# Second attention layer: q and k rows turned by VectorE and sent through DRAM in place of TensorE transpositions

## The reference, cut to what matters

```python
q = (hidden_states @ Wq + bq).reshape(b, n, H, HD)     # b = 2, n = 512, H = 32, HD = 128
k = (hidden_states @ Wk + bk).reshape(b, n, H, HD)
v = (hidden_states @ Wv + bv).reshape(b, n, H, HD)
q = rmsnorm(q, gq)                                     # over each head's 128 numbers
k = rmsnorm(k, gk)
scores = jnp.einsum('bnhd,bmhd->bhnm', q, k) * scale
attn = jax.nn.softmax(scores, axis=-1)
out = jnp.einsum('bhnm,bmhd->bnhd', attn, v).reshape(b, n, H * HD)
return out @ Wo + bo
```

## Time and profile before

| | us |
|---|---|
| median of the runs | 2196.71 |
| the profiled execution | 2198.5 |
| its span | 2196.7 |
| first attention layer and what follows it, about | 0 to 840 |
| second attention layer, about | 840 to 1950 |
| last feed-forward, about | 1950 to 2197 |

### The profile page before, as it was taken

The page is one execution under the profiler, slowest core; times in us unless marked ns, Lnnn a source line. Parts: engine busy times, 40 slices in busy tenths (PEclk is TensorE's granted clock), DMA queues, the critical chain, the costliest instruction groups (busy, mean ns, idle before and its releaser), DMA issues. The chain is left out here.

```text
span 2196.7 us, 37916 instructions
## 1 busy us (share of the span) xinstructions
PE 2089.8 (95%) x10535; PEld 1757.2 (80%) x10535; DVE 1636.8 (75%) x2972; ACT 1348.5 (61%) x3637; POOL 1222.3 (56%) x985
## 2 busy tenths in 40 slices
PE   6999999999999879999999999999999999868998
PEld 4788888888888657888888888888888888756786
DVE  6778888888788776778777777777777787775422
ACT  5777777777776455656566565666656665544321
POOL 3878778787786554546454554545445463354300
PEclk9999999999999989999999999999999999979999
DMA  2644444434444513555454455444554444643210
GB/s 83 131 105 126 108 110 114 115 104 127 102 119 129 140 55 69 105 122 114 114 108 104 109 119 115 109 99 111 118 115 111 99 111 93 142 95 105 87 53 25
DMA packets 219135, 231.69 MB, mean 105 GB/s; under 512 B 100528, under 2 KB 130384, under 8 KB 218992
## 3 DMA queue, kind: packets, MB, share of 16 engines
q1 hardware_dynamic: 218992, 229.97, 43.7%
HBM read 114.23 MB, written 6.55 MB: 55 GB/s over the span
## 5 line engine op out<-in xcount | busy, mean ns | idle before, releaser
L90 POOL TENSOR_TENSOR l_probsT_lo<-l_moved,l_probsT_hi 128x512 fp32r<-128x512 f32 (+2 forms) x256 | 280.4, 1100 | 296.7 <-ACT l_probsT_hi L947 269.2
L941 ACT ACTIVATE l_probs<-l_score,l_negtop 128x512 f32<-128x512 f32 x256 | 175.8, 687 | 373.2 <-DVE l_negtop L1052 359.9
L90 DVE TENSOR_TENSOR l_probsT_lo<-l_moved,l_probsT_hi 128x512 fp32r<-128x512 f32 (+1 forms) x256 | 292.5, 1143 | 37.4 <-ACT l_probsT_hi L947 37.0
L1052 DVE TENSOR_REDUCE l_negtop<-l_score 128x1 f32<-128x512 f32 x256 | 175.7, 687 | 93.1 <-PE l_score L85 90.6
L1833 ACT ACTIVATE l_probs<-l_score,l_negtop 128x128 f32<-128x128 f32 (+3 forms) x256 | 134.7, 526 | 170.3 <-DVE l_negtop L1946 169.4
L83 PE MATMUL l_out<-l_w_out_lo,l_oT_hi 128*128 128x512 f32 x512 | 209.0, 408 | 6.2 <-DVE l_oT_lo L1078 4.0
L83 PE MATMUL l_score<-l_kT_lo,l_qT_hi 128*128 128x512 f32 (+3 forms) x512 | 191.0, 373 | 22.4 <-POOL l_qT_lo L90 8.9
L1946 DVE CUSTOM_DVE_ANT_0 l_score<-l_score,l_mask 128x128 f32<-128x128 f32 (+3 forms) x256 | 125.9, 492 | 106.9 <-PE l_score L85 105.5
L84 PE MATMUL l_out<-l_w_out_hi,l_oT_lo 128*128 128x512 f32 x512 | 201.7, 394 | 0.0
L85 PE MATMUL l_out<-l_w_out_hi,l_oT_hi 128*128 128x512 f32 x512 | 201.5, 393 | 0.0
L83 PE MATMUL l_general<-l_w_qk_lo,xT_hi 128*128 128x512 f32 x504 | 198.1, 393 | 2.5 <-PEq L1452 2.5
(11 more groups left out here) (249 smaller groups left out, 6235.7 us busy)
## 6 DMA issues: line engine op xcount, KB each, us to landing
l_moved<-l_blocks SPq DMA_DIRECT2D x1024, 64.0 KB
l_moved<-l_blocks SPq DMA_DIRECT2D x512, 80.0 KB
l_inv_all<-inv_rows SPq DMA_DIRECT2D x32, 512.0 KB
l_raw_out<-l_wo SPq DMA_DIRECT2D x64, 256.0 KB, 4.3
l_inv_all<-inv_rows SPq DMA_DIRECT2D x64, 256.0 KB
l_raw_q<-l_wq SPq DMA_DIRECT2D x32, 256.0 KB, 4.0
l_raw_qk<-l_wq SPq DMA_DIRECT2D x64, 128.0 KB, 2.8
l_raw_qk<-l_wk SPq DMA_DIRECT2D x64, 128.0 KB, 2.9
```

What stands on the lines that cost most here:

```text
L90: return engine.tensor_tensor(out, full, hi.bitcast(F32), ALU.subtract)
L941: act.activation(probs[:, n % NPR], score[n % 2][:], ACT.Exp, bias=negtop[:, n:n + 1], accum_out=total[:, n:n + 1]).then_inc(s_exp, 1)
L1052: dve.tensor_reduce(negtop[:, n:n + 1], score[n % 2][:], AXX, ALU.max, negate=True)\
```

## The change

The eight TensorE uses "tq" and "tk" of a turn go. In their place, per unit: VectorE turns the four scaled y tiles in blocks of 32 x 32 into `y_blocks` (`TURNS1`, steps -7 and -6 of the unit, two each, at the end of VectorE's step). SyncE sends them to a DRAM tensor `y_rows` in four transfers of 256 KB (`SENDS1`, step -5), and takes them back per slot in two transfers of 256 KB in turned order (`TAKES1`, step -4 of an even slot, -5 of an odd one), as soon as all four transfers of the send have landed and TensorE has made the last score that reads the buffer. ScalarE makes the high halves out of the landed rows (`HALVES1`, step -2 or -3) and scales k's rows in place, GpSimd subtracts for the low halves, which lie in the place of the landed rows. In a step, sends and takes stand on SyncE between the biases and `move`. The score product reads the keys through `by_tile`, in runs of 32 numbers, since their order is now another. The first unit's two slots are still turned by TensorE, ahead of the loop, into the banks of scores and outputs (`turn_first`, `first_hi`, `first_lo`). The bias buffer has one place instead of two, so its load waits for the last y tile of the turn before and moves to step -17. Smaller edits: semaphores are shared between uses (in the block before and in the last feed-forward, counts adjusted), and the loads of the last stage wait for the turned rows in place of the last transposition's bank.

```diff
-USES1 |= {(kind, s): 4 * s + n for kind, n in (("tq", -4), ("tk", -3), ("pv", PV_AT)) for s in range(SLOTS)}
-USES1 = Plan(USES1, lambda x: ("y", "v", "tq", "tk", "pv").index(x[0]))
+USES1 |= {("pv", s): 4 * s + PV_AT for s in range(SLOTS)}
+USES1 = Plan(USES1, lambda x: ("y", "v", "pv").index(x[0]))
+TURNS1 = Plan({(r, b, t): 16 * r + 8 * b - 7 + t // 2 for r, b in PAIRS for t in range(TB)}, lambda x: x)
+SENDS1 = Plan({(r, b): 16 * r + 8 * b - 5 for r, b in PAIRS})
+TAKES1 = Plan({(s,): 4 * s - (4, 5)[s % 2] for s in range(SLOTS)})
+HALVES1 = Plan({(kind, s): 4 * s - (2, 3)[s % 2] for kind in QK for s in range(SLOTS)})
...
-BIAS1 = Plan({(r,): 16 * r - 22 for r in range(2)})
-
-
-def of_halved(x):
-    return x[0] in ("v", "tq", "tk")
+BIAS1 = Plan({(r,): 16 * r - 17 for r in range(2)})
...
-        qT = split("qT", [P, 2, S])
-        kT = split("kT", [P, 2, S])
+        with ExitStack() as early:
+            turned = p.sb(early, "l1_turned", [P, 2, 2, S])
+        qk_lo = sb("qk_lo", [P, 2, 2, S], F32R)
+        qT, kT = (Split(sb(f"{kind}T_hi", [P, 2, S], F32R), qk_lo[:, k]) for k, kind in enumerate(QK))
...
+        y_blocks = sb("y_blocks", [P, 4, C, P])
...
+        def first_turned(h, kind):
+            return (score, out_bank)[h][kind == "k"]
...
+        def by_hand(m, d, slot):
+
+            return m.first and d == 0 and slot < 2
...
+        def item_of(x):
+            return turned[:, QK.index(x[0]), x[1] % 2]
+
+        def by_tile(rows):
+            return rows.rearrange("p (g t i) -> p t g i", g=TB, t=TB)
...
+            def send_rows(m, unit, d):
+                if not (m.first and m.number(SENDS1, unit, d) <= 3):
+                    sp.wait_ge(s_y_in, y_taken(m, pair_slots(*unit)[1], d, 4))
+                    sp.nop(nofuse=True)
+                if not (m.first and m.number(SENDS1, unit, d) <= 2):
+                    sp.wait_ge(s_y_sent, y_sent(m, unit, d, 1))
+                    sp.nop(nofuse=True)
+                sp.wait_ge(s_y_block, m.done(TURNS1, (*unit, TB - 1), d) - TB)
+                sp.nop(nofuse=True)
+                for g in range(TB):
+                    sp.dma_start(y_rows[unit[1], g].rearrange("n c i x -> i (n c) x"),
+                                 y_blocks[32 * g:32 * g + 32].rearrange("p n c x -> p (n c) x")).then_inc(s_y_sent, 16)
+
+            def take_rows(m, slot, d):
+                r, b, h = pair_of(slot)
+                sp.wait_ge(s_y_sent, y_sent(m, (r, b), d))
+                sp.nop(nofuse=True)
+                if not (m.first and slot == 2):
+                    sp.wait_ge(s_y_in, y_taken(m, slot, d, 1))
+                    sp.nop(nofuse=True)
+                sp.wait_ge(s_score, (m.i + d) * TILES + TB * (slot - 1))
+                sp.nop(nofuse=True)
+                for k in range(2):
+                    sp.dma_start(turned[:, k, h].rearrange("p (g x) -> p g x", g=TB),
+                                 y_rows[b, :, h + 2 * k].rearrange("g c i x -> (c i) g x")).then_inc(s_y_in, 16)
...
+                    for x, d in m.turns(SENDS1, n):
+                        send_rows(m, x, d)
+                    for x, d in m.turns(TAKES1, n):
+                        if not by_hand(m, d, x[0]):
+                            take_rows(m, x[0], d)
...
-                elif kind in ("tq", "tk"):
-                    r, b, h = pair_of(x[1])
-                    if kind == "tq" and h == 0:
-                        pe.wait_ge(s_yn, m.done(USES1, ("y", r, b, TB - 1), d, of_y))
-                    at = (h + 2 * (kind == "tk")) * HD
-                    for t in range(TB):
-                        last = pe.transpose(bank[:, t * P:(t + 1) * P], y[:, b, t, at:at + HD], ident[:])
...
-                            pe.wait_ge(s_free, m.done(USES1, ("tk", slot)))
+                            pe.wait_ge(s_qk_lo, m.done(HALVES1, ("k", slot)))
                         wait_past(pe, s_exp, m, TILES, n - 1)
-                        product(nc, score[n % 2][:], qT[:, slot % 2, t * P:(t + 1) * P], kT[:, slot % 2])\
+                        keys = Split(by_tile(kT.hi[:, slot % 2]), by_tile(kT.lo[:, slot % 2]))
+                        product(nc, tokens(score[n % 2][:]), qT[:, slot % 2, t * P:(t + 1) * P], keys)\
...
+            def rows_hi(x, m, d):
+                kind, s = x
+                act.wait_ge(s_y_in, y_taken(m, s, d))
+                if kind == "q":
+                    last = act.activation(qT.hi[:, s % 2], item_of(x), ACT.Copy)
                 else:
-                    act.activation(kT.hi[:, x[1] % 2], bank[:], ACT.Copy, scale=gains[:, 2:3]).then_inc(s_bank_hi, 1)
+                    act.activation(kT.hi[:, s % 2], item_of(x), ACT.Copy, scale=gains[:, 2:3])
+                    last = act.activation(item_of(x), item_of(x), ACT.Copy, scale=gains[:, 2:3])
+                last.then_inc(s_qk_hi, 1)
...
-                elif kind == "tq":
-                    last = rest(dve, qT.lo[:, x[1] % 2], bank[:], qT.hi[:, x[1] % 2])
-                elif kind == "tk":
-                    last = dve.scalar_tensor_tensor(kT.lo[:, x[1] % 2], bank[:], gains[:, 2:3],
-                                                    kT.hi[:, x[1] % 2].bitcast(F32), ALU.mult, ALU.subtract)
...
+            def turn_rows(m, x, d):
+                r, b, t = x
+                if t == 0:
+                    if not (m.first and m.number(SENDS1, (r, b), d) <= 2):
+                        dve.wait_ge(s_y_sent, y_sent(m, (r, b), d, 1))
+                        dve.nop(nofuse=True)
+                dve.wait_ge(s_yn, m.done(USES1, ("y", r, b, t), d, of_y))
+                to = y_blocks[:, :, :, 32 * t:32 * t + 32]
+                dve.transpose(to, y[:, b, t]).then_inc(s_y_block, 1)
...
+            def rows_lo(x, m, d):
+                kind, s = x
+                pool.wait_ge(s_qk_hi, m.done(HALVES1, x, d))
+                to = (qT if kind == "q" else kT)[:, s % 2]
+                rest(pool, to.lo, item_of(x), to.hi).then_inc(s_qk_lo, 1)
...
+        y_rows = nc.dram_tensor("y_rows", [B, TB, 4, C, 32, P], F32, kind="Internal").ap()
...
```

More of the change, by code:

```diff
@@ L599, in load_bias @@
     def load_bias(self, sp):
[L600 to L604 removed]
+        for e in range(2):
+            rows = self.a[("l1_bq", "l1_bk")[e]][0:1, 0:2 * HD]
+            sp.dma_start(self.b_qk[:, e * 2 * HD:(e + 1) * 2 * HD], rows.to_broadcast([P, 2 * HD]))\
+                .then_inc(self.s_b, 16)
         for k, n in enumerate(("l1_gq", "l1_gk")):
@@ L657, in scalar, with paired_attention @@
                 self.square(act, 0, t)
-def paired_attention(p, ctx0, xT, acc, ident, half, inv_rows, ahead, entry):
+def paired_attention(p, ctx0, xT, acc, ident, half, inv_rows, y_rows, ahead, entry):
     nc, a = p.nc, p.a
@@ L706, in paired_attention @@
         s_w_hi, s_w = ahead.s_w_hi, ahead.s_w
-        s_const, s_zero, s_bv = ahead.s_const, sem("zero"), sem("bv")
+        s_const, s_set = ahead.s_const, sem("set")
         s_b = ahead.s_b
@@ L1005, in bank_use @@
                         dve.nop(nofuse=True)
-                        dve.wait_ge(s_b[r], (m.i + d + 1) * 32)
-                    if t == 0 and m is not start and not (m.first and d == 0 and r == 0):
-                        dve.nop(nofuse=True)
-                        dve.wait_ge(s_bank, m.done(USES1, ("tk", pair_slots(1 - r, b)[1]), d - (r == 0)))
-                    last = dve.tensor_tensor(y[:, b, t], bank[:], b_qk[:, r], ALU.add)
+                        dve.wait_ge(s_b, (m.i + d) * 64 + 32 * (r + 1))
+                    last = dve.tensor_tensor(y[:, b, t], bank[:], b_qk[:], ALU.add)
                 elif kind == "v":
@@ L1149, in body @@
                             landed_lo(m, slot, k)
+                    for x, d in m.turns(HALVES1, n):
+                        if not by_hand(m, d, x[1]):
+                            rows_lo(x, m, d)
                     for x, d in m.turns(USES1, n, 2):
@@ L2299, in build @@
         grouped_attention(p, ctx, xT, acc, ident, half, x_rows, kept, inv_rows[0], ahead)
-        paired_attention(p, ctx, xT, acc, ident, half, inv_rows[1], ahead, entry)
+        paired_attention(p, ctx, xT, acc, ident, half, inv_rows[1], y_rows, ahead, entry)
         swiglu_phase(p, ctx, xT, xT_words, acc, kept, out_rows, entry)
```

168 lines of the change are left out of this document (97 added, 71 removed).

## The result

| | before | after |
|---|---|---|
| median of the runs, us | 2196.45 (one chip, side by side) | 2376.07 (2372.95 to 2383.56, 4 runs) |
| span of the profiled execution, us | 2196.7 | 2371.1 |
| mean of the same 14 turns, us | 69.5 | 80.6 |

The changed kernel is slower, ratio 1.0818 with the interval [1.0789, 1.0847], 180 us where I had forecast 56. The direction and the place were right, the size was not: 2376 lies outside the range of 2185 to 2305.

What follows compares the result with a forecast made beforehand. TensorE was taken to bound the second layer at 69.65 us a turn; after the change SyncE would, at 59.9 + 9.4 + 4.2 = 73.5. Fifteen turns at +3.85 make +58, ends -3: 2252 us predicted, range 2185 to 2305.

Steps and rivals of the forecast that it cites:

- SyncE decides, and TensorE's saving is lost behind it: Second attention layer: SyncE's queue at 73.5 us a turn sets the pace, against TensorE's 66.1; chance 0.62.
- SyncE's load of before, 59.9 us a turn: SyncE's queue in the second layer: occupied 59.9 us of a 69.65 us turn before the change, free for 9.7.
- Sends, 9.4 us a turn: SyncE's queue: two sends a turn, 4.7 us each from first issue to landing, 9.4 us (6.8 to 15).
- Rival 2: Second layer: the data path is the bound, with slow landings; 79.1 us a turn, +142 us, 2339 us; chance 0.12.
- the sum's high end, 80.3 us: SyncE's turn in the second layer with the high ends of sends and takes: 80.3 us, +160 us.
- Takes, 4.2 us a turn: SyncE's queue: four takes a turn, each two issues plus small waits, 1.05 us each, 4.2 us (3.0 to 5.4).
- The loop is shorter than SyncE's time: Send, landing, take, halves and TensorE's steps to the sums: 30.7 us for eight steps, against SyncE's 36.8.
- TensorE's need 66.1 us: TensorE in a second-layer turn: 69.65 falls to 66.1 us without "tq" and "tk", score products costing nothing more.
- Ends, -3 us: Last twelve steps with only TensorE's saving left, and small start and end effects of the layer: together -3 us.
- Clock: TensorE idling some 10% of a turn: clock 0.95 would make 66.1 us 69.6, still under SyncE; cost left at zero.
- VectorE blocked by GpSimd: Second layer: VectorE standing still for GpSimd's new 10.3 us would reach 65 us a turn, under TensorE's 66.
- The signs that I had named: Changed profile: TensorE about 90%, waiting for k's lows; SyncE waiting at every send, hardly for inverses; turn about 73.5 us.

Runs made afterwards that it cites:

- e1: The kernel before with only SyncE's new sends and takes added, into a buffer nobody reads, TensorE still turning q and k: 2416.2 us, ratio 1.1028.
- e4: The changed kernel with each send carrying a quarter of its bytes, one column block read four times: 2298.1 us, ratio 1.0478.
- e17: The changed kernel with each send writing its 256 KB as 32 runs of 8 KB instead of 512 runs of 512 B: 2369.8 us, ratio 1.0807.
- e2: The changed kernel with each take reading the rows of the unit before, so none waits for a fresh landing: 2304.2 us, ratio 1.0485.
- e3: The changed kernel with SyncE's passes written out instead of looped: 2335.1 us, ratio 1.064.
- e12: The changed kernel with the even slot's take put behind the move of the same step in SyncE's queue: 2541.9 us, ratio 1.1572.
- e9: The changed kernel with SyncE's passes written out and weights fetched in 4 transfers a turn instead of 14: 2352.5 us, ratio 1.0712.
- e14: The changed kernel with passes written out, weight fetches merged, and a quarter of the bytes in the sends: 2271.2 us.
- e18: The changed kernel with passes written out, weight fetches merged, weights behind the sends, and longer runs for sends and takes: 2288.4 us, ratio 1.044.
- e16: The changed kernel with passes written out, weight fetches merged, takes of the unit before's rows, and quarter-byte sends: 2199.4 us, ratio 1.0012.
- e7: The changed kernel with GpSimd's new subtractions replaced by writes of zeros, low halves left out: 2387.1 us, ratio 1.0839.

## Why the prediction was wrong, point by point

- **SyncE decides, and TensorE's saving is lost behind it.** Right: e1 loses all of it with the arithmetic of before, and taking the landing wait, the bytes or the loop edge away each gives some back.
- **SyncE's load of before, 59.9 us a turn.** Right, 59.3 in the changed kernel.
- **Sends, 9.4 us a turn.** This is the step that failed. I took the four issues and the landing of 1 MB as one quiet store of 1 MB, 4.4 us, and 0.48 us an issue from weights that come in. Measured: 14.2 us. Both halves were small: the issues are 0.8 us apart, and a 256 KB transfer lands 4.4 us after its issue (median). The sum also left out most of its own issues: three more at 0.48 us in front of a landing of 4.4 are 5.8 us, not 4.7. Still, 5.8 is short of 7.1. I had the better row in hand, the 7.5 us of the store that goes out beside another, and gave it to the rival as an upper end. The sends are 4.8 us of the 7.3 by which the turn was too short. Rival 2, with its 79.1 us a turn and 2339 us, was the nearest of my cases, and its chance of 0.12 too small. Its mechanism was right in this: the time is that of the bytes (e4, e17). Its other half is not borne out: takes land in 3.7 us, not in 5 to 6. The measured turn is at the sum's high end, 80.3 us, which my range left out. The Trainium skill's page (SBUF — State Buffer, Door 1: The DMA port swizzle) gave, by my estimate, some 6 us and was closer than my sum; no run here tells whether the ports are the reason.
- **Takes, 4.2 us a turn.** Measured 5.2. The two issues last 0.93 us, as I had them; the rest is time between them and the next inverse. A slower issue behind a send shows only where the landing is not waited for (e2).
- **A term that was not in the sum: SyncE's loop edge**, some 6 us in every second turn, five in the layer, 2.1 us in the mean of a turn; writing the passes out gave 41 us (e3). No row could have given it: in the kernel before, the queue has no gap over 3.4 us at that place. Why the edge is longer in the changed kernel stays open.
- **The loop is shorter than SyncE's time: 30.7 against 36.8 us.** The order was right, the length not. The estimate from e12 is 35.7 us, with 40.4 for SyncE. In the changed kernel SyncE waits for no other engine in the 700 us; in e9 for 1.9 us, in e14 for 8.3, in e18 for 32. So the loop shows only where SyncE's own part has become short.
- **TensorE's need 66.1 us.** 67.5 by the estimate from e16, so 2.1 of the 3.5 us. That the score products cost no more with their runs of 32 numbers was right: 397 to 402 ns in e16, at full clock, against 392 to 424 before.
- **Ends, -3 us.** Measured +19, of which one turn's loss of 3.85 us was in the forecast: 14.8 us up to the second fetch of v's weights and 4 behind the last; +13 in e16. In the layer's start SyncE stands 13.6 us at the bias load, whose wait I had put at nothing, and 10.2 us at the first send, for VectorE's turnings. TensorE is busy 100.6 us between 820 and 940 us (106.3 in e16), where it had 113.0. The first unit's own detour was sized at nothing.
- **Clock.** 0.95 in the turns, where 1.00 was granted while TensorE was full. That it decides nothing as long as SyncE is the pace is argued from the sums; e16, where TensorE is at 98%, has it back at 1.00.
- **VectorE blocked by GpSimd.** No effect: e7 takes GpSimd's new reads away and gains nothing.

The signs that I had named were there: TensorE at 87% instead of about 90, the low halves of k as its wait, a landing wait at every send, no wait for inverses. Only the number that I gave for the turn was off.

## What to carry to other kernels

A store that is waited for in an in-order queue costs the whole time until it has landed, and that is set by the bytes under way at that moment, its own and those handed over just ahead of it: price it by the slowest comparable transfer of the trace, not by the quiet one, and price the issue with it. Before adding to a queue that looks free, add up its occupied time at the places where the work would go, and leave room for a stall that no row of the old kernel shows, such as the loop edge here. Count what a relief takes away from the transfers in the trace: the ten issues a turn that I took for twenty were there to be counted. And compare the second-longest ring with the first: here it is, by estimate, 12% behind, at 71.4 us a turn, and so above the 69.5 of the kernel before even with SyncE's queue made shorter.

## What the runs showed of the hardware

- The price of issuing a transfer on SyncE is not fixed: 0.46 us apart for 64 KB sends, 0.8 us for the same sends with 256 KB, 0.69 us for tiny transfers in the changed kernel.
- 1 MB out of SBUF in four transfers takes 7.1 us from its first issue to the take that waits for it in runs of 512 B, and 6.8 us in runs of 8 KB (e17).
- Merging 14 fetches into 4, same bytes, moved the landing of the sends behind them from 4.8 to 6.1 us after their issue (e3, e9), and the kernel from 2335.1 to 2352.5 us.
- In the changed kernel SyncE's loop has an edge of 5.5 to 6.4 us in which it issues nothing; written out, it is gone (e3). With the transfers of e1 it is 3.8 to 4.1 us, against 2.3 to 2.6 at the other boundaries.
- Eight tiny transfers a turn on a queue with 14% free time slowed a kernel that is bound by TensorE by 1.6%.
